# Moving one pair of head transposes from the end of a batch's first quad to its second quad

## The reference

```
xn = layernorm(x)
q, k, v = xn @ Wq.T, xn @ Wk.T, xn @ Wv.T            # 16 heads of 16
A = tril(taylor_exp(q) . taylor_exp(k))              # 1 + s + s^2/2 of the scaled score s
y = (A @ v) / (row sum of A)                         # per head
x + y @ Wo.T + moe(xn)                               # 8 experts, 2 per token, SwiGLU, 256 -> 512 -> 256
```

## Time and profile before

| what | value |
|---|---|
| median of 3 runs | 671.7 us (670.17 to 672.0) |
| the profiled execution | 669.97 us, span 668.2 us |
| PE busy | 640.6 us, 96% of the span |
| DVE busy | 409.9 us, 61% |
| ACT busy | 341.9 us, 51% |
| POOL busy | 344.1 us, 51% |
| mean granted clock of PE | 0.984 |

### The profile page before, as it was taken

One profiled execution on the slowest core, in us unless ns is written; L12 is line 12 of the kernel. 1 busy time (PEld: TensorE's weight loads), 2 busy tenths in 40 slices (PEclk: granted clock), 3 DMA queues, 4 the chain that ended last, 5 costly groups with the idle time before them and its releaser, 6 DMA issues.

```text
span 668.2 us, 16297 instructions
## 1 busy us (share of the span) xinstructions
PE 640.6 (96%) x5351; PEld 493.3 (74%) x5351; DVE 409.9 (61%) x1067; ACT 341.9 (51%) x515; POOL 344.1 (51%) x381
## 2 busy tenths in 40 slices
PE   8799999999999999888999999999999999999994
PEld 6465666666666666546888888888888888888883
DVE  6776878787878585785984445444444544444452
ACT  3577878787877686764653223232322323232231
POOL 3255555546463736463464555555555545455542
PEclk9799999999999999987999999999999999999998
DMA  4643555455434435447533333334342333333332
GB/s 133 143 121 105 123 158 129 151 128 162 81 109 107 124 89 159 113 143 274 179 59 59 51 65 50 61 55 66 51 66 50 57 58 52 64 52 64 52 49 24
DMA packets 37773, 64.05 MB, mean 96 GB/s; under 512 B 8288, under 2 KB 25824, under 8 KB 37696
## 3 DMA queue, kind: packets, MB, share of 16 engines
q0 software_dynamic: 16704, 28.12, 21.4%
q1 hardware_dynamic: 20432, 34.24, 20.1%
q10 hardware_dynamic: 560, 0.66, 0.3%
HBM read 27.72 MB, written 22.68 MB: 75 GB/s over the span
## 4 chain that ended last, share of the span: by engine, by line
PE 87%; DVE 6%; ACT 2%; DMA 2%; issue 2%; ACTq 0%; POOL 0%; POOLq 0%; DVEq 0%
PE banks L1173 30%; PE banks L1194 15%; PE banks L1053 10%; PE banks L1035 8%; PE banks L1073 7%; PE banks L1182 5%; PE banks L1082 4%; PE banks L1117 4%; PE banks L1162 2%; PE banks L1102 1%; ACT T L530 1%; PE banks L1108 1%; DVE xTl L737 1%; PE banks L1091 1%; DMA out<-yo,xw 1%
## 5 line engine op out<-in xcount | busy, mean ns | idle before, releaser
L493 POOL DMA_INDIRECT out<-yo,xw x71 | 112.2, 1581 | 155.7 <-DVE yo L993 102.3
L622 ACT ACTIVATE sTh<-banks 128x512 fp32r<-128x512 f32 x71 | 42.5, 598 | 192.3 <-PE banks L1182 192.3
L473 POOL TENSOR_SCALAR_AFFINE_SELECT T<-T 128x512 f32<-128x512 f32 x128 | 80.6, 641 | 109.9 <-ACT T L536 41.7
L985 DVE TENSOR_TENSOR sTl<-banks,sTh 128x512 fp32r<-128x512 f32 x71 | 49.0, 691 | 118.0 <-ACT sTh L622 118.0
L1173 PE MATMUL banks<-w12h,xgh 128*128 x284 | 118.5, 417 | 0.9 <-DVE xgl L976 0.9
L1173 PE MATMUL banks<-w12l,xgh 128*128 x284 | 112.8, 397 | 0.0
L1173 PE MATMUL banks<-w12h,xgl 128*128 x284 | 112.6, 396 | 0.0
L482 POOL DMA_INDIRECT xg<-xs_scr,glist x71 | 73.4, 1033 | 21.5 <-issue 19.0
L1053 PE MATMUL banks<-T,vau 128*17 128x512 f32 (+3 forms) x1024 | 77.2, 441 | 0.2 <-POOL T L473 0.2
L1035 PE MATMUL banks<-Q,K 32*128 32x256 f32 (+2 forms) x1024 | 71.2, 363 | 6.0 <-DMA K<-Kt 2.8
L464 POOL DMA_INDIRECT xs_scr<-xb,slots x64 | 63.5, 993 | 18.8 <-issue 10.0
(11 more groups left out here) (172 smaller groups left out, 1212.6 us busy)
## 6 DMA issues: line engine op xcount, KB each, us to landing
Q<-Q SPq DMA_DIRECT2D x128, 64.0 KB, 2.3
w12r<-w SPq DMA_DIRECT2D x16, 512.0 KB, 4.8
out<-xa SPq DMA_DIRECT2D x16, 256.0 KB, 2.5
w3r<-w SPq DMA_DIRECT2D x8, 512.0 KB, 7.1
K<-Kt SPq DMA_DIRECT2D x124, 32.0 KB
xa<-x SPq DMA_DIRECT2D x7, 512.0 KB, 4.7
xg<-xs_scr,glist POOLq DMA_INDIRECT x71, 2.9
out<-yo,xw POOLq DMA_INDIRECT x71, 3.8
```

Source lines behind the costliest of these rows:

```text
L473: e.affine_select(out=v, in_=v, pattern=[[0, 4], [1, P]], compare_op=ALU.is_ge, fill=-1.0, base=0, channel_multiplier=-1).then_inc(s["g_mk ...
L493: e.indirect_dma_start(out, bass.IndirectOffsetOnAxis(xw[:, t % 4, NE:NE + 1].bitcast(U32), 0), yo[:, t % 2, :], None, compute_op=ALU.add) ...
L985: e.tensor_tensor(sTl[:], banks[:, 5, :], sTh[:].bitcast(F32), ALU.subtract).then_inc(s["v_st"], 1)
```

## The change

In the batches 1 to 6 the step `("y", b - 1, 1)` leaves slot c of quad 0, where it stood between `c3` and `r`, and goes to slot c of quad 1, ahead of `("c", b + 1, 0)`. In the last batch it stays where it was. Since PE, ACT and DVE all walk `slot_c(n)`, the step moves on all three, and since `misc_uses()` is made from the same lists, the banks of the steps between the two places are dealt anew: the list becomes `T, c2, t3', c3, r` and `x0, x1, t0, y1', c0, v0, v1`.

```diff
     b, qd = divmod(n, 4)
     if qd == 0:
-        return [("c", b, 3)] + ([("y", b - 1, 1)] if b else []) + [("r", b, 0)]
+        return [("c", b, 3)] + ([("y", b - 1, 1)] if b == LAST else []) + [("r", b, 0)]
     if b == LAST:
         return [("y", b, 0)] if qd == 3 else []
     if qd == 3:
         return ([("o", b - 1, 1)] if b else []) + [("y", b, 0), ("C", b + 1, 0)]
-    return ([("c", b + 1, 0)] if qd == 1 else []) + [("v", b + 1, 2 * qd - 2), ("v", b + 1, 2 * qd - 1)]
+    steps = [("y", b - 1, 1)] if b and qd == 1 else []
+    return steps + ([("c", b + 1, 0)] if qd == 1 else []) + [("v", b + 1, 2 * qd - 2), ("v", b + 1, 2 * qd - 1)]
```

## The result

The changed kernel takes 677.18 us (median of 3 runs, 676.73 to 677.31) against 671.7 us (670.17 to 672.0): a ratio of 1.0089, 95% interval 1.0066 to 1.0111. It is 6.0 us slower by the ratio (4.4 to 7.5), 5.5 by the two medians, and 677.1 was forecast. The profiled execution took 677.31 us, with a span of 675.5.

What follows compares the result with a forecast made beforehand. PE was taken to set the pace, busy 34.43 of 35.00 us per batch. Terms of -0.39, +0.5, +0.07 and +0.82 made +1.03 per batch, +6.2 over six batches on 670.9: 677.1 us, range 673.8 to 680.0.

Steps and rivals of the forecast that it cites:

- Quad 0: Where the step leaves, r inherits y's wait for DVE's Q; next scores come 0.39 us earlier, at most 0.49.
- The gap is not filled: Quad 1: y1' waits for x0's bank as c0 did, so the 0.52 us idle stays, now ahead of y1'.
- c0: Quad 1: c0 needs x1's release and starts at 139.96, some 0.07 us more than y leaves.
- the sum: Per batch -0.39 (quad 0), +0.5 (y in quad 1), +0.07 (c0), +0.82 (v1): +1.03 us; over six batches +6.2.
- The wait of v1: Quad 1: v1 needs y1''s bank, released by `yTl`, which DVE makes behind `place_rows`; PE waits 0.82 us.
- Given back: Behind v1: DVE is on time again and no later PE gap takes up the loss, so it reaches the end.
- The bounds: Limits of v1's wait: both L819 instructions at their fastest give +3.1 us; 0.1 more DVE backlog per batch gives +6.8.
- the main case: v1 waits for `yTl` in quad 1; alone it holds 674.0 to 679.5 us; chance 0.72.
- The clock: Rival: the new 0.82 us gap soon after the old lowers PE's clock; 688 us for six falls, 679 for one; chance 0.12.
- a filled gap: Rival: y1' does not need x0's bank and lies wholly in the 0.52 gap; -3.1 us; chance 0.06.
- `yTl` in time: Rival: `yTl` is ready before v1 needs the bank, leaving about +0.2 us per batch, +1 us; chance 0.10.

Runs made afterwards that it cites:

- ytl_first: The changed kernel with, in DVE's order in quad 1, the moved step's `yTl` made ahead of `place_rows` instead of behind it: 672.2 us, ratio 1.0012.
- y_after_c0: The changed kernel with the moved step behind c0 instead of ahead of it: 681.83 us, ratio 1.0157.
- x0_early: The kernel before with x0 moved, on PE and ACT, ahead of the second part of quad 1's scores; DVE's order stays: 670.66 us, ratio 0.9988.

## Why the prediction was right

Taken by its own steps, in batch 3:

- **Quad 0.** From the start of c3's last product to the next scores it was 0.95 us (132.31 to 133.26) and is 0.49 (134.33 to 134.82): a gain of 0.46, where 0.39 was taken and 0.49 was the upper bound. r did inherit y's wait for Q, but the scores follow its weight load by about 0.2, not 0.31.
- **The gap is not filled.** From those scores to the end of the gap it is 6.48 us (134.82 to 141.30) against 6.49: y1' stands where c0 stood, with the same 0.52 ahead of it.
- **c0.** It starts 0.60 behind y1', as the sum had it (139.36 to 139.96).
- **The wait of v1.** v0 to v1 takes 1.56 (143.39 to 144.95) against 0.73: 0.83, where 0.82 was forecast. The list of waits calls it 0.67, since it counts from the modelled end of the last product. From the first `xTl` to the start of `yTl` DVE takes 3.64 us (140.56 to 144.20), where 3.65 was taken. ytl_first shows the cause of the wait and y_after_c0 its rule.
- **Not in the sum.** v1 to the scores of quad 2 takes 0.92 against 0.82. The rest of the batch, from there to the next `T`, is 20.69 (145.87 to 166.56) against 20.55 (142.80 to 163.35); the first scores of quad 3, 0.90 instead of 0.74, are most of that. They wait inside for the square of ACT that ended quad 2: their third product starts at 154.16, 0.05 behind that square's end (154.11). ACT began those squares (L537) at 152.60, 1.21 behind their scores, where it was 0.77 before (148.33 to 149.10), because the semaphore of the scores came 1.18 us behind the scores' start instead of 0.75; why it came later is not shown. The two add 0.24 to the 1.03, and quad 0's larger gain takes 0.07 off; batch 3 is +1.17 (36.26 against 35.09) and the mean +1.15.
- **Given back.** Nothing is: DVE is on time again at the next attention sum, and no later gap shrinks.
- **The bounds.** The range of the main case does not follow from its own terms: +6.8 us on the slowest execution shown (672.0) is 678.8, not 679.5. Nothing hangs on it here.
- **The clock.** It stays at 1.00 in the batch shown, with gaps of 0.52 and 0.67 within 4 us, and in y_after_c0 with a gap of 1.28 to 1.39 in each batch besides the one of 0.52 or 0.88. So the length of one gap does not explain the fall in the last batch, which the prediction priced behind a gap of 0.99. The rival falls, and so do those with a filled gap and with `yTl` in time.

The price of the whole was sized at 6.2 and came as 6.0 by the times of the runs and 6.9 by the batches of the profiled ones. The mechanism and its main term are shown. That the time came within 0.1 us of 677.1 is luck: the executions of the kernel before spread over 2 us, and the sum lacked 0.24 us behind v1 in batch 3.

## What to carry to other kernels

Where steps take buffers in turn, moving one step moves every wait between its old and its new place. Count which step releases the buffer that each one takes, and on which engine and behind what that release is queued. A gap ahead of a step can't be filled by work that needs the same buffer, and when the gap's chain runs through another engine, freeing the buffer sooner may only move the wait, as it did in x0_early. Before moving work into a gap, check both its entry (what lets it start there) and its exit (who needs its buffer next): here the entry gained nothing and the exit cost 0.8 us in each batch but the first.

## What the runs showed of the hardware

**A new start of PE's products.** Behind its wait, v1's second product starts 0.22 us after the first instead of 0.12 (144.95 and 145.17), and v1 as a whole takes 0.92 instead of 0.82, in the change and in y_after_c0. In ytl_first, without the wait, it takes 0.82 again. The 0.1 us is not a mark of a wait alone: v2, straight behind scores and with no wait listed, has it in the kernel before too (113.91 and 114.14).

**DVE while POOL masks.** DVE's small product (L820, 128x32) took 0.56 and 0.33 us at its place in batch 3 of the change, but 0.28 and 0.19 in ytl_first. What goes with it is how long POOL's masking (L474) ran at the same time. In the traces of the kernel before, the change, ytl_first and y_after_c0 the product takes 0.19 us with POOL not masking, 0.18 to 0.28 with 0.1 to 0.26 us of masking beside it, 0.33 or 0.34 with 0.29, and 0.56 or 0.57 with 0.6. No run moved the masking alone, so the cause is not shown, but it is about half a microsecond of the work that stood ahead of `yTl`. The lower bound of the wait, which the prediction took from two such products at their fastest, would need POOL not to mask at that time.
